# A decoder layer on one core: queries taken by VectorE, the cross output projection in split products, the expert-tile plan made early

## The reference

```python
# self-attention, 16 heads of 32, after a layer norm xn
q, k, v, p, y = split(xn @ W_in.T + b_in, [512, 1024, 1536, 2048])   # y: 16 columns
k = (1 - smear) * k + smear * k_prev
pos = cumsum(sigmoid(y)^T)
scores = q k^T / (s*s*sqrt(32)) + causal - (pos_i - pos_j)
out = (silu(p) * (softmax(scores) @ v)) @ W_out.T                # then layer norm
x = LN(x + out)
# cross attention, 16 heads of 64; keys and values from [LN(ctx), LN(x)], 512 of them
x = LN(x + softmax(q k^T, masked) v @ Wout)                      # Wout: 1024 x 256
# mixture of 8 experts, the best 2 for each token
x = LN(x + sum over the two of gate * (gelu(x W1 + b1) W2 + b2))
```

## Time and profile before

| | us |
|---|---|
| three runs, median | 2685.38 |
| lowest, highest | 2684.51, 2691.44 |
| the profiled execution | 2680.88 |
| its span in the trace | 2679.0 |

### The profile page before, as it was taken

The page is one execution under the profiler, slowest core; times in us unless marked ns, Lnnn a source line. Parts: engine busy times, 40 slices in busy tenths (PEclk is TensorE's granted clock), DMA queues, the critical chain, the costliest instruction groups (busy, mean ns, idle before and its releaser), DMA issues. The chain is left out here.

```text
span 2679.0 us, 61019 instructions
## 1 busy us (share of the span) xinstructions
PE 2382.6 (89%) x17865; PEld 1973.1 (74%) x17865; DVE 1817.7 (68%) x5239; ACT 1727.8 (64%) x4347; POOL 936.7 (35%) x983
## 2 busy tenths in 40 slices
PE   4888888885799999999999999999999379999991
PEld 3777777774677777777777777777776379999991
DVE  4766767665567666766677666766676268787776
ACT  3888888885466666666566656666566156676662
POOL 3454444444432233223332233223331134444434
PEclk8999999998899999999999999999999689999995
DMA  5644555453000000000000000000000166767766
GB/s 124 176 112 113 125 129 112 110 117 86 24 10 16 17 17 1 16 17 17 9 9 16 17 17 1 16 17 17 9 8 9 61 216 230 244 230 229 244 219 196
DMA packets 160229, 224.40 MB, mean 84 GB/s; under 512 B 33872, under 2 KB 127696, under 8 KB 159568
## 3 DMA queue, kind: packets, MB, share of 16 engines
q1 hardware_dynamic: 149040, 201.88, 26.8%
q0 software_dynamic: 9664, 20.53, 2.3%
q10 hardware_dynamic: 1376, 0.54, 0.1%
HBM read 140.15 MB, written 24.01 MB: 61 GB/s over the span
## 5 line engine op out<-in xcount | busy, mean ns | idle before, releaser
L1517 DVE CUSTOM_DVE_ANT_0 x_prob<-x_score,x_mask_add 128x512 f32<-128x512 f32 x512 | 348.1, 682 | 282.7 <-PE x_score L1748 226.7
L1320 ACT ACTIVATE x_prob<-x_prob,x_low 128x512 f32<-128x512 f32 x512 | 366.5, 718 | 199.4 <-DVE x_low L1517 195.6
L1326 ACT COPY x_pt<-x_ptb 128x512 f32<-128x512 f32 x512 | 272.9, 584 | 244.3 <-PE x_ptb L1760 243.4
L1241 POOL TENSOR_TENSOR x_k_lo<-x_whole,x_k_hi 128x512 fp32r<-128x512 f32 x128 | 165.9, 1296 | 413.7 <-ACT x_k_hi L1366 411.3
L1528 DVE TENSOR_SCALAR x_prob<-x_prob,x_rden 128x512 f32<-128x512 f32 x512 | 272.9, 574 | 0.6
L1760 PE MATMUL x_ptb<-ident,x_prob 128*128 128x128 f32 x2048 | 267.7, 274 | 2.6 <-PEq L1791 2.3
L484 ACT ACTIVATE prob<-prob,low 128x128 f32<-128x128 f32 (+1 forms) x512 | 233.5, 468 | 54.9 <-DVE low L727 53.8
L1777 PE MATMUL x_av<-x_pt,x_vx 128*64 128x256 f32 x2048 | 249.3, 385 | 0.8 <-ACT x_pt L1326 0.8
L1760 PEld LDWEIGHTS x_ptb<-ident,x_prob 128*128 128x128 f32 x2048 | 230.6, 141 | 14.3 <-issue 11.6
L1497 DVE COPY x_whole<-x_proj 128x512 f32<-128x512 f32 x192 | 130.8, 687 | 130.5 <-PE x_proj L1681 128.5
L1777 PEld LDWEIGHTS x_av<-x_pt,x_vx 128*64 128x64 f32 x2048 | 135.9, 136 | 100.1 <-issue 44.8
(11 more groups left out here) (276 smaller groups left out, 7246.7 us busy)
## 6 DMA issues: line engine op xcount, KB each, us to landing
w_s<-w SPq DMA_DIRECT2D x156, 512.0 KB
k_parts<-k_hi SPq DMA_DIRECT2D x128, 128.0 KB, 2.4
q_parts<-q_hi SPq DMA_DIRECT2D x128, 128.0 KB, 2.4
k_parts<-pos_parts SPq DMA_DIRECT2D x128, 64.0 KB, 2.4
k_parts<-k_lo SPq DMA_DIRECT2D x64, 128.0 KB, 2.4
q_parts<-q_lo SPq DMA_DIRECT2D x64, 128.0 KB, 2.4
w_s<-expert_rows SPq DMA_DIRECT2D x16, 512.0 KB, 4.7
b_s<-b SPq DMA_DIRECT2D x39, 128.0 KB
```

The lines of the kernel that those rows point to most:

```text
L1241: pool.tensor_tensor(part_of(n, q_lo, k_lo), whole_of(n), part_of(n, q_hi, k_hi).bitcast(F32), ALU.subtract).then_inc(low_ready.sem, 1)
L1320: nc.scalar.activation(slot, slot, ACT.Exp, bias=low[:, u:u + 1], scale=-1.0, accum_out=den[:, u:u + 1]).then_inc(exp_ready.sem, 1)
L1326: nc.scalar.copy(pt[:, u % PX_RING, :], ptb[u % 2][:, :]).then_inc(pt_taken[u % 2].sem, 1)
L1517: dve.tensor_tensor_reduce(prob[:, u % PROB_RING, :], score[u % 2][:, :], mask_add[:, :], -X_SCALE, 3.0e38, ALU.add, ALU.min, low[:, u:u + ...
```

## The change

- Self phase: VectorE takes the queries from PSUM into `q_t` (`take_q`, four tensor_scalar), ScalarE makes `q_hi` from `q_t` with one cast for each pair (`high_q`). y becomes six split products of 256 columns in step 3. ScalarE copies transposed probabilities ahead of the other parts of a step. VectorE's and ScalarE's steps are dealt out anew; among them `x_stats(b+1)` goes from step 10 to step 4, `place_pos` from 9 to 10, `silu` from 8 to 11, `residual_sum` from 11 to 10.
- Cross phase: the output projection is made pair by pair (`output(b, m)`, six split products each) into a PSUM bank of its own, pairs 0 to 5 in steps 8 to 18, pairs 6 and 7 in steps 0 and 1 of the next iteration. ScalarE writes `ox` and `ox_hi`, GpSimd `ox_lo`; `wox` is split ahead of the loop, and its memory is used for probabilities. The values have one bank in place of two. The prefixes take fp32r operands.
- The plan of expert tiles is made at the end of the cross phase's VectorE program. SyncE's queue waits for the last scatter in place of the plan, and GpSimd no longer waits for it at the end of its cross program.

The core of the diff:

```diff
 # self phase, ScalarE
-            def take_q(b, n, i):
+            def high_q(b, n):
                 f = QP + n
-                if n == 0 and i == 0:
+                if n == 0:
                     act.wait_ge(q_split.sem, q_split.at(b - 1, 2))
-                filled(b, f)
-                m = 2 * n + i
-                for dst in (q_t, q_hi):
-                    ins = nc.scalar.activation(dst[:, m, :], proj[f % 2][:, i * S:(i + 1) * S], ACT.Identity,
-                                               bias=q_bias[:, m:m + 1], scale=q_scale[:, m:m + 1])
-                if i == 1:
-                    taken(ins, f)
+                act.wait_ge(proj_taken[f % 2].sem, proj_taken[f % 2].at(b, f // 2 + 1))
+                nc.scalar.copy(q_hi[:, 2 * n:2 * n + 2, :], q_t[:, 2 * n:2 * n + 2, :]).then_inc(q_hi_ready.sem, 1)
...
-            steps = {1: [take_xt], 3: [take_y], 4: [lambda b: smear_k(b, 0)], 5: [lambda b: smear_k(b, 1)], 6: [lambda b: high_k(b, 0)],
-                     7: [lambda b: high_k(b, 1), lambda b: take_q(b, 0, 0)], 8: [lambda b: take_q(b, 0, 1)], 9: [lambda b: take_q(b, 1, 0)],
-                     10: [lambda b: take_q(b, 1, 1), take_output(0)], 11: [take_output(1)], 13: [lambda b: tanh_p(b, 0)],
-                     14: [lambda b: tanh_p(b, 1)]}
+            steps = {1: [take_xt], 4: [take_y, lambda b: smear_k(b, 0)], 5: [lambda b: smear_k(b, 1)], 6: [lambda b: high_k(b, 0)],
+                     7: [lambda b: high_k(b, 1)], 9: [lambda b: high_q(b, 0)], 10: [lambda b: high_q(b, 1), take_output(0)],
+                     11: [take_output(1)], 13: [lambda b: tanh_p(b, 0)], 14: [lambda b: tanh_p(b, 1)]}
...
                     exps(b, i)
+                    take_transposed(*unit(b, i - COPY_LAG))
                     for part in parts.get(i, ()):
                         part(b)
-                    take_transposed(*unit(b, i - COPY_LAG))
 # self phase, VectorE
+            def take_q(b, n):
+                f = QP + n
+                if n == 0:
+                    dve.wait_ge(q_split.sem, q_split.at(b - 1, 2))
+                filled(b, f)
+                for i in range(2):
+                    m = 2 * n + i
+                    ins = dve.tensor_scalar(q_t[:, m, :], proj[f % 2][:, i * S:(i + 1) * S],
+                                            q_scale[:, m:m + 1], q_bias[:, m:m + 1], ALU.mult, ALU.add)
+                taken(ins, f)
...
-                     4: [lambda b: one_over_sums(b, 0), forget_gates],
+                     4: [lambda b: one_over_sums(b, 0), lambda b: x_stats(b + 1)],
                      5: [lambda b: widen(b, 0), lambda b: gate(b - 1, 3)],
-                     6: [lambda b: take_k(b, 0), lambda b: centred(b - 1)],
-                     7: [lambda b: take_k(b, 1)],
-                     8: [lambda b: one_over_sums(b, 1), silu],
-                     9: [lambda b: widen(b, 1), place_pos],
-                     10: [lambda b: x_stats(b + 1)],
-                     11: [lambda b: residual_sum(b - 1)],
+                     6: [lambda b: take_k(b, 0), forget_gates],
+                     7: [lambda b: take_k(b, 1), lambda b: centred(b - 1)],
+                     8: [lambda b: one_over_sums(b, 1), lambda b: take_q(b, 0)],
+                     9: [lambda b: widen(b, 1), lambda b: take_q(b, 1)],
+                     10: [lambda b: residual_sum(b - 1), place_pos],
+                     11: [silu],
...
 # self phase, TensorE
             def project_y(b):
                 bk_ = free(b, YP)
-                in_sbuf(b, XT)
-                full(project(bk_[0:HEADS, 0:S], lambda k: win_y[:, k, :], lambda k: xn_t[:, k, :], KC))
+                pe.wait_ge(xn_split.sem, xn_split.at(b, 1))
+                full(project_parts(bk_[0:HEADS, 0:S], lambda a, k: (win_y_hi, win_y_lo)[a][:, k, :],
+                                   lambda a, k: xn_parts[a][:, k, :]))
...
 # cross phase, TensorE
-            def output(b):
-
-                bk_ = free(b, WOX)
-                for i in range(2):
-                    pe.wait_ge(av_taken[i].sem, av_taken[i].at(b - 1, XC // 2))
+            def output(b, m):
+
+                pe.wait_ge(ox_ready.sem, ox_ready.at(b, m + 1))
+                if m == 0:
+                    pe.wait_ge(residual_ready.sem, residual_ready.at(b, 1))
                 for c in range(TC):
-                    ins = project(bk_[:, c * D:(c + 1) * D], lambda k: ox_t[:, k, c * P:(c + 1) * P], lambda k: wox[:, k, :], XC)
-                full(ins)
+                    for i, j in ((0, 0), (0, 1), (1, 0)):
+                        ins = matmul(out_sum[:, c * D:(c + 1) * D], (ox_hi, ox_lo)[i][:, m % 2, c * P:(c + 1) * P],
+                                     (wox_hi, wox_lo)[j][:, m, :], start=(m + c + i + j == 0), stop=(m == XC - 1 and c == 1 and i == 1))
+                ins.then_inc(out_done.sem, 1)
...
+                    if i == 0:
+                        output(b - 1, XC - 2)
+                    elif i >= 8 and i % 2 == 0:
+                        output(b, (i - 8) // 2)
...
 # expert phase, SyncE's queue
-            sp.wait_ge(plan, N_PLAN)
+            sp.wait_ge(scattered.sem, scattered.at(B, scattered.per))
```

More of the change, by code:

```diff
@@ L557, in projections @@
                 for n in range(2):
-                    for i in range(2):
-                        take_q(b, n, i)
+                    high_q(b, n)
                 for n in range(2):
@@ L774, in _ @@
             for n in range(2):
+                take_q(-1, n)
+            for n in range(2):
                 half_p(-1, n)
@@ L1093, in cross_phase @@
         ptb = [bank(f"ptb{i}") for i in range(2)]
-        av = [bank(f"av{i}") for i in range(2)]
+        av, out_sum = bank("av"), bank("out_sum")
         consts, consts_v = sem("x_consts"), sem("x_consts_v")
@@ L1127, in cross_phase @@
         av_done = signal("av_done", XC)
-        av_taken = [signal(f"av_taken{i}", XC // 2) for i in range(2)]
+        av_taken, ox_ready, out_done = signal("av_taken", XC), signal("ox_ready", XC), signal("out_done", XC)
         route_steps, margin_steps = signal("route_steps", 14), signal("margin_steps", 1)
@@ L1142, in whole_of, with prob_slot @@
             return whole[:, n % WHOLES, :].rearrange("p (i s) -> p i s", i=2)
+        def prob_slot(u):
+            n, first = u % PROB_RING, XC * D // N_KEYS
+            return first_probs[:, n, :] if n < first else more_probs[:, n - first, :]
         def part_of(n, q, k):
@@ L1295, in _ @@
             next_tokens(B - 1)
+            for m in range(3):
+                low_ox(B - 1, m)
             slots_known(B - 1)
@@ L1386, in _ @@
             take_latents(-1)
+            nc.scalar.copy(wox_hi[:], wox[:]).then_inc(weights_hi, 1)
+            for hi, whole_ in ((ox_hi, ox), (ox_lo, ox), (before_hi, before), (ones_hi, ones)):
+                nc.scalar.copy(hi[:], whole_[:])
             for f in range(LT + 1, FILLS):
@@ L1502, in take_v @@
                 dve.wait_ge(av_done.sem, av_done.at(*last))
-                taken(dve.tensor_copy(vx[:, n, 512 * half:512 * (half + 1)], proj[f % 2][:, :]), f)
+                ins = dve.tensor_copy(vx[:, n, 512 * half:512 * (half + 1)], proj[f % 2][:, :])
+                ins.then_inc(proj_taken[f % 2].sem, 2 if f == NONE - 2 else 1)
             def spread_mask(b):
@@ L1630, in _, with step @@
             dve.tensor_tensor(counts[:], next_free[:], expert_base[:], ALU.subtract).then_inc(counts_ready, 1)
+            def step(ins, n):
+                ins.then_inc(plan, 1)
+                dve.wait_ge(plan, n)
+            dve.wait_ge(counts_ready, 1)
+            step(dve.tensor_tensor(has_tile[:], counts[:].unsqueeze(2).broadcast_to([P, E, MAX_TILES]),
+                                   bound[:].unsqueeze(1).broadcast_to([P, E, MAX_TILES]), ALU.is_gt), 1)
+            step(dve.tensor_reduce(tiles_of[:], has_tile[:], AX_X, ALU.add), 2)
+            step(dve.tensor_tensor_scan(last_tile[:], one_e[:], tiles_of[:], 0.0, ALU.mult, ALU.add), 3)
+            step(dve.tensor_tensor(is_past[:], tile_no[:].unsqueeze(2).broadcast_to([P, N_TILES, E]),
+                                   last_tile[:].unsqueeze(1).broadcast_to([P, N_TILES, E]), ALU.is_ge), 4)
+            step(dve.tensor_tensor(past_tiles[:], is_past[:], tiles_of[:].unsqueeze(1).broadcast_to([P, N_TILES, E]),
+                                   ALU.mult), 5)
+            step(dve.tensor_reduce(expert_f[:], is_past[:], AX_X, ALU.add), 6)
+            step(dve.tensor_reduce(first_f[:], past_tiles[:], AX_X, ALU.add), 7)
+            dve.tensor_scalar(expert_rows_f[:], expert_f[:], float(REGION), None, ALU.mult)
+            step(dve.tensor_tensor(first_f[:], tile_no[:], first_f[:], ALU.subtract), 8)
+            dve.tensor_scalar(tile_expert[:], expert_f[:], float(E - 1), None, ALU.min)
+            step(dve.scalar_tensor_tensor(out=expert_rows_f[:], in0=first_f[:], scalar=float(SLOTS), in1=expert_rows_f[:],
+                                          op0=ALU.mult, op1=ALU.add), 9)
```

(5 more changed lines are left out.)

204 lines of the change are left out of this document (107 added, 97 removed).

## The result

The changed kernel takes 2778.24 us (median of 4 runs, 2773.26 to 2778.55) against 2686.22 (4 runs, 2684.51 to 2691.44): ratio 1.0338, 95% interval 1.0325 to 1.0352. It is slower, inside the range of 2700 to 2800, 30 us above the forecast of 2748. The profiled execution took 2778.18 us with a span of 2776.4, 97.4 more than before.

The account below looks back on a forecast made before the run. Bounds: order of steps and waits between engines in the self phase, with its queue nearly full; TensorE in the cross phase. Self +64, cross +6, expert start -5 gave +65, forecast 2748 us, range 2700 to 2800.

Parts of the forecast that it names:

- The mechanism: Self phase: x_stats in step 4 waits 5 to 7 us for x_raw every iteration; loads 39 to 42 us apart.
- the cycle: Self loop: load, statistics, steps 4 to 10, positions, 34 queue issues, next load; its length is the period, 40.8 us.
- D: Self loop: VectorE's time from x_stats' start in step 4 to pos_parts' end in step 10, taken as 14.8 us.
- The fixed part: Self loop: the share of the period independent of engines, queue issuing, load landing and semaphore, 26.0 us.
- the gap for the split queries: SyncE's queue in the self loop: its 2.6 us wait before q_hi would go, as ScalarE makes q_hi earlier.
- my floor of 12.7: Self loop, x_stats to pos_parts: VectorE's time if it never waits, 12.7 us; a rival at 12.7 to 14 had 0.24.
- ScalarE's relief: Self loop: ScalarE loses eight activations and gets two casts, -3.5 us, which cuts VectorE's waits for scores.
- the rival in which it stays low until the values: Self phase: TensorE's clock stays low after each stall, D 16 to 17.8, 2768 to 2795 us; chance 0.15.
- About -4 us per iteration: Self phase: what its other edits would gain per iteration if the queue's cycle did not bind.
- the rival that I gave 0.09: Self phase: the queue doesn't bind, so about -4 us per iteration comes out, 2621 to 2625 us; chance 0.09.
- Cross phase: Output projection moved into TensorE's full steps: +0.7 us per iteration, +6 in all (-29 to +15).
- Start of the expert phase: The plan's VectorE operations move before the barrier, ahead of the tokens' load: -5 us (-6 to -3.7).

Follow-up runs that it names:

- Experiments 1: The changed kernel with x_stats(b+1) moved back from step 4 to step 10, behind place_pos: 2688.87 us, ratio 1.001.
- experiment 2: The changed kernel with the next x_raw load issued between the second and third spread of SyncE's queue, x_stats left in step 4: 2672.01 us, ratio 0.995.
- experiment 3: The kernel before the change with only x_stats(b+1) moved from step 10 to step 4: 2722.71 us, ratio 1.0132.
- 4: The changed kernel with place_pos moved from the end of step 10 to the end of step 9: 2738.97 us, ratio 1.0197.
- experiment 5: The changed kernel with GpSimd's subtraction that makes q_lo left out in the loop: 2737.57 us, ratio 1.0184.
- experiment 7: The changed kernel with the early x_raw load and y made in plain fp32 in step 2, not as split products: 2647.81 us, ratio 0.9847.
- experiment 8: The changed kernel with the early x_raw load and place_pos moved from step 10 to step 9: 2664.06 us, ratio 0.9916.
- experiments 6: The changed kernel with the whole self phase of the kernel before, cross and expert phases as changed: 2675.64 us, ratio 0.9942.
- 10: Changed self phase with early x_raw load and plain fp32 y, cross and expert phases of the kernel before: 2658.14 us, ratio 0.9894.

## Why the prediction was right, and which of its numbers were off

**The mechanism** held in each link: x_stats waits for x_raw in every iteration, the queue issues without a gap from the positions to the load, 43.9 us are the sum of the parts. The loads lie 43.6 us apart on average, over the 39 to 42 that I had named. Experiments 1 and 2 open the cycle in two places and both take the loss away; 3 closes it in the other kernel; 4 and 5 shorten one link and the period follows. By experiment 3 the move of x_stats alone costs 37 of the 92 us. The other edits add to it chiefly by a longer D, 17.4 us over the passes against 12.1 there.

**The fixed part** was 26.0 in the prediction (23.2 + 2.7 + 0.1) and is 26.1. That the gap for the split queries goes was right. So was the idle time of x_stats in kind; it is 8.0 us, over the 5 to 7 that I had named.

**The term that was mis-sized is D**, "I take D = 14.8": it is 17.8, at the far end of my bounds. Over the loop it is 43.56 - 26.1 = 17.5, and 15 x (17.5 - 14.8) = 40 is the whole error of the self phase, 105.2 - 64 = 41. The window of the stretch shown, columns as in the earlier trace rows:

```profile
340.74:358.54 17.80, 14.24 (x90) 12.99 (x90) 15.21 (x49) 11.28 (x37) 5.38 (x5) 0.72 0.00 0
```

VectorE is busy 15.2 us of the 17.8 and idle 2.6. Of the busy time I had not priced 2.9 us at all, in which its operations with two inputs in SBUF stood still beside GpSimd: 0.70 in centred, 1.08 in residual_sum, 1.12 in pos_parts. Without them its work is 12.3, 0.4 under my floor of 12.7. The idle 2.6 are 0.5 more than the 2.1 that 14.8 left for waiting: 0.53 and 1.66 of them are for scores. ScalarE's relief doesn't show in them; TensorE, at half its clock until 350.80, is late with the score that VectorE waits 1.66 us for.

The mean durations of the earlier trace rows were right for the old order, where these operations lay beside nothing of GpSimd's; the change put two of them beside q_lo and centred beside k_lo. Experiment 5 shows this for the 2.2 us of the last two; for centred it is read from traces alone. Who starts first matters there: in experiment 2's trace centred starts together with k_lo, at 340.49, and takes 0.86 us, while the two k_lo take 3.25 us, where two of them alone take 2.56. The Trainium skill, "SBUF — State Buffer", section "Who interferes with whom", says that a VectorE instruction with two SBUF inputs contends with a GpSimd instruction that reads SBUF, and that the one that issues first keeps the shared pair of ports for its whole instruction while the other blocks. The traces agree: the ends lie 0.27 and 0.28 us behind GpSimd's, and with GpSimd silent the operations take 0.88 and 0.41. With the 2.2 us of those two, my D would have been 17.0.

**The clock** fell as forecast, to 0.50 in 342.73 to 350.80, and the rival in which it stays low until the values came nearest: its 2768 to 2795 us hold the measured time. That is in part luck. It raised D to 16 to 17.8 by the low clock alone, while 2.9 of the 3.0 us above my 14.8 stand beside GpSimd, which no rival of mine named. No run was made to isolate what the clock costs in the changed kernel. In experiment 3, in the other kernel, the stretch is 1.7 to 2.4 us longer in passes with a fall than in those without. The changed kernel has no pass without one, and its D doesn't follow the length of the low stretch (some 6.8 us low in passes with a D of 16.6, 17.3 and 18.0), so the size there stays open. The Trainium skill's rule on loops that wait for a DMA in every pass ("TensorE: Matmul & The Clock Gate", "HAM oscillation — how this bites in real kernels") agrees with the changed kernel's trace, where all 15 passes start on the low clock or fall to it. In experiment 3 the loop waits for its DMA in every pass too, 1.7 us and more, but only eight of fifteen show the fall behind it.

**"About -4 us per iteration" without the cycle**, the gain of the rival that I gave 0.09, was too much by far. With the load out of the way the changed order gains 0.7 us a period (36.48 against 37.14), not 4. One reason is shown by experiment 7: y as split products waits 2.15 us for xn_lo, so the 2.27 for pt went and another wait took its place; undone, the period falls by 1.7. Another is the place of the position write beside q_lo: moved away from there it gives some 8 us in all (experiment 8). So even where the queue did not bind, 2625 us were not to be had from this edit as it stands; experiment 2's 2672 are what it gives.

**Cross phase**: forecast +6, measured about 0. The loop costs +0.5 us an iteration (+0.7 forecast), 7.7 us over fifteen; the end of the phase, with the block that stood uncovered, saves the other 5.8 (-6); the prologue took 0.8 less, not 1 more; the fp32r prefixes save 1.2 once more at the end. **Start of the expert phase**: -6.0 (-5). A further -1.8 lies in the tiles themselves; its cause was not looked for. By medians of runs (experiments 6 and 10) the rest of the change is worth -10 to -13 rather than the -8 of two traces; that difference stays open.

## What to carry to other kernels

When a consumer moves ahead in an order, ask which queue entry brings its data, and what that queue's next entries wait for: a load behind 34 issues of 0.6 us, which start only after the consumer's own engine has gone on, makes a loop of its own, and its length can be summed from the trace before anything is built. Break it at the cheapest place, which here was one DMA moved ahead on the queue, not the statistics moved back. And price an operation in its new neighbourhood: durations from the old order hold only if the same engines run beside it.

## What the runs showed of the hardware

- A VectorE operation with two SBUF inputs that starts behind a subtraction of GpSimd's, or during one, ends about 0.27 us after it: 0.41 us became 1.53, a pair of 0.88 became 1.96, and both were back with that subtraction left out (experiment 5). Where centred started together with k_lo it kept its 0.86 us and GpSimd took longer (experiment 2).
- The issue of a DMA costs its queue 0.59 us for each spread of 128 KB and 0.39 for a load of 256 KB; the 34 issues are 23.35 us of a loop of 43.6, with the DMA engines busy 44% of the time.
- A wait of 8.0 us of VectorE, which left TensorE 4.60 us without work, was followed by 8 us at a granted clock of 0.50. Behind shorter idle times of TensorE it went either way: after 1.86 us the clock stayed at 1.00 in one pass of experiment 3 and fell to 0.50 in another, and the stretch from x_stats to the positions took 1.7 to 2.4 us more in its passes with a fall.
